# A vision layer's token product in native fp32 throughout, with its 64 tail features once

## What is computed

```
h = einsum('bnd,de->bne', patches(x), W) + b        # 768 -> 192
qkv = h @ w_qkv.T                                   # 192 -> 3 * 768
...
h = _layernorm(h + (scores @ v) @ w_out.T + b_out)
h = _layernorm(h + moe(h))
```

## Time and profile before

| | |
|---|---|
| runs | 155.52 us median (154.16 to 157.65) |
| the profiled execution | 152.08 us, span 150.4 us |
| TensorE busy | 141.0 us, 94% of the span, granted clock 0.995 |
| VectorE, ScalarE, GpSimd busy | 106.0, 95.2, 87.0 us |
| DMA | 10.60 MB, mean 71 GB/s |

### The profile page before, as it was taken

How to read it: one execution, slowest core, us unless ns; L and a number is a source line. 1 busy time by engine, 2 the same in 40 slices (tenths; PEclk the granted TensorE clock), 3 DMA queues, 4 the chain that set the end, 5 groups by cost and what they waited for, 6 DMA issues and landing times. The chain is left out here.

```text
span 150.4 us, 3231 instructions
## 1 busy us (share of the span) xinstructions
PE 141.0 (94%) x1155; PEld 127.3 (85%) x1156; DVE 106.0 (70%) x248; ACT 95.2 (63%) x215; POOL 87.0 (58%) x99
## 2 busy tenths in 40 slices
PE   6999899999999899999979999999999999999960
PEld 2779799999966578798858898999999998999950
DVE  0037889269378879999876538779768797678852
ACT  3055989985498896768688988225555545444531
POOL 7701169590448686899997657737625434433602
PEclk9999999999999999999999999999999999999998
DMA  5899999810033000203300000000000000000021
GB/s 139 261 399 255 247 313 248 226 43 0 3 106 107 2 4 10 97 4 105 109 0 0 0 4 2 0 2 4 0 0 0 0 4 0 0 2 4 0 66 52
DMA packets 4511, 10.60 MB, mean 71 GB/s; under 512 B 592, under 2 KB 1424, under 8 KB 4496
## 3 DMA queue, kind: packets, MB, share of 16 engines
q1 hardware_dynamic: 4496, 10.41, 24.2%
HBM read 9.96 MB, written 0.44 MB: 69 GB/s over the span
## 5 line engine op out<-in xcount | busy, mean ns | idle before, releaser
L462 POOL TENSOR_TENSOR reg_r<-reg_p,reg_r 128x324 fp32r<-128x324 f32 (+1 forms) x23 | 19.1, 832 | 20.6 <-ACT reg_r L721 20.6
L382 POOL TENSOR_TENSOR reg_w<-stage,reg_w 128x768 fp32r<-128x768 f32 x12 | 22.5, 1884 | 12.8 <-DVE reg_q L903 4.5
L721 ACT ACTIVATE reg_r<-reg_p 128x324 fp32r<-128x324 f32 (+1 forms) x24 | 10.6, 443 | 23.9 <-DVE reg_p L1076 23.8
L1053 DVE TENSOR_SCALAR reg_q<-ps,bup 128x324 f32<-128x324 f32 (+1 forms) x24 | 12.3, 513 | 5.3 <-PE ps L1290 5.1
L1076 DVE SCALAR_TENSOR_TENSOR reg_p<-reg_q 128x324 f32<-128x324 f32 (+1 forms) x24 | 13.8, 575 | 2.2
L1286 PE MATMUL ps<-reg_r,reg_w 128*128 128x324 f32 (+1 forms) x48 | 14.9, 311 | 0.0
L1289 PE MATMUL ps<-reg_r,reg_w 128*128 128x324 f32 (+1 forms) x48 | 14.2, 296 | 0.0
L1287 PE MATMUL ps<-reg_r,reg_w 128*128 128x324 f32 (+1 forms) x48 | 14.2, 296 | 0.0
L1290 PE MATMUL ps<-reg_r,reg_w 128*128 128x324 f32 (+1 forms) x48 | 14.2, 296 | 0.0
L1288 PE MATMUL ps<-reg_r,reg_w 128*128 128x324 f32 (+1 forms) x48 | 14.2, 295 | 0.0
L528 ACT ACTIVATE reg_w<-stage 128x768 fp32r<-128x768 f32 x13 | 10.9, 841 | 2.5 <-DMA stage<-w_qkv_a 1.1
(11 more groups left out here) (217 smaller groups left out, 452.6 us busy)
## 6 DMA issues: line engine op xcount, KB each, us to landing
reg_x<-xw_in SPq DMA_DIRECT2D x5, 416.0 KB, 6.4
stage<-w_gu_a SPq DMA_DIRECT2D x4, 384.0 KB, 5.6
stage<-w_gu_b SPq DMA_DIRECT2D x8, 192.0 KB, 3.8
stage<-w_qkv_a SPq DMA_DIRECT2D x3, 384.0 KB, 9.1
stage<-w_qkv_b SPq DMA_DIRECT2D x6, 192.0 KB, 9.2
stage<-w_down SPq DMA_DIRECT2D x3, 384.0 KB, 3.2
wout<-w_out SPq DMA_DIRECT2D x1, 576.0 KB, 11.8
reg_x<-xw_in SPq DMA_DIRECT2D x1, 272.0 KB, 2.8
```

Of the source, the lines that this page charges most:

```text
L382: nc.gpsimd.tensor_tensor(dst[:, 1, :], raw, f(dst[:, 0, :]), ALU.subtract).then_inc(s_wlop, 1)
L462: nc.gpsimd.tensor_tensor(acts[:, n % NACT, 1, 0:w], act_f[:, n % 4, 0:w], f(acts[:, n % NACT, 0, 0:w]), ALU.subtract).then_inc(s_alo, 1)
L1053: nc.vector.tensor_scalar(upw[:, n % 4, 0:w], ps[:, e_bank(n) + 1, 0:w], bup1[:, c:c + 1], LIMIT + 1, ALU.add, ALU.min).then_inc(s_u, 1)
```

## The change

- Chunks 3 to 5 are multiplied natively as well; the split copies `xw`, `x_hi` and `x_lo` go, and so do 36 split products.
- The weights hold the 64 tail columns once: a row has `WX` = 192 + 576 = 768 columns. The tail product of the first token half goes to partitions 0 to 63 of bank 6, that of the second half to partitions 64 to 127 of bank 7, as two products of 64 columns each for every chunk.
- Since each tail half now stands on one half of the partitions only, it is moved when it is evacuated. ScalarE writes the first half's hi in place, the second half's hi in place (partitions 64 to 127, as input of the low part) and once more to partitions 0 to 63; VectorE writes both low parts to partitions 64 to 127, one after the other.
- `hT[:, 0]` is evacuated in two halves: tokens 0 to 287 by ScalarE, 288 to 575 by VectorE, with a semaphore of its own (`s_hthid`). `first_units` goes through token half 0 first and waits for the second half's semaphore before half 1.
- `hb`'s tail has 64 partitions and two instructions; `project`'s second transpose has 64 columns and 64 rows.
- SP issues `small` behind piece 0.

```diff
-XW = T + 2 * 128
+XW = T + D
-WX = 2 * 128
+WX = D
...
-            sp.dma_start(sm[:, :], small).then_inc(s_small, 16)
             for k in range(len(pieces)):
...
+                if k == 0:
+                    sp.dma_start(sm[:, :], small).then_inc(s_small, 16)
...
-            for t in range(2):
-                act.wait_ge(s_tok, t + 1)
-                nc.scalar.activation(two(hT[:, t]), halves(4 + 2 * t), ACT.Identity,
-                                     bias=sm[:, C_TOKB + t:C_TOKB + t + 1]).then_inc(s_hthi, 1)
+            def tail_bias(dst, a, bias):
+
+                r = slice(64 * a, 64 * a + 64)
+                return nc.scalar.activation(dst, ps[r, 6 + a, 0:TH], ACT.Identity, bias=bias[r])
+
+            tail_b = sm[:, C_TOKB + 1:C_TOKB + 2]
+            act.wait_ge(s_tok, 1)
+            nc.scalar.activation(hT[:, 0, 0:TH], ps[:, 4, 0:TH], ACT.Identity, bias=sm[:, C_TOKB:C_TOKB + 1])\
+                .then_inc(s_hthi, 1)
+            act.wait_ge(s_tok, 2)
+            tail_bias(hT[0:64, 1, 0:TH], 0, tail_b).then_inc(s_hthi, 1)
+            tail_bias(hT[64:128, 1, TH:T], 1, tail_b).then_inc(s_hthi, 1)
+            tail_bias(hT[0:64, 1, TH:T], 1, tail_b).then_inc(s_hthi, 1)
...
+            act.wait_ge(s_htlo, 1)
+            act.wait_ge(s_smprep, 3)
+            nc.scalar.activation(two(hb[:, 0]), halves(4), ACT.Identity, bias=tbo[:, 0:1]).then_inc(s_hb, 1)
+            act.wait_ge(s_htlo, 3)
+            tail_bias(hb[0:64, 1, 0:TH], 0, tbo[:, 1:2])
+            tail_bias(hb[0:64, 1, TH:T], 1, tbo[:, 1:2]).then_inc(s_hb, 1)
...
+            dve.wait_ge(s_tok, 1)
+            nc.vector.tensor_scalar(hT[:, 0, TH:T], ps[:, 5, 0:TH], sm[:, C_TOKB:C_TOKB + 1], None, ALU.add)\
+                .then_inc(s_hthid, 1)
+            dve.wait_ge(s_hthid, 1)
             dve.wait_ge(s_hthi, 1)
...
-            dve.wait_ge(s_hthi, 2)
-            nc.vector.scalar_tensor_tensor(out=two(hT[up, 1]), in0=ps[up, 6:8, 0:TH],
-                                           scalar=sm[up, C_TOKB + 1:C_TOKB + 2], in1=two(f(hT[up, 1])),
-                                           op0=ALU.add, op1=ALU.subtract).then_inc(s_htlo, 1)
+            for a in range(2):
+                r = slice(64 * a, 64 * a + 64)
+                cols = slice(TH * a, TH * a + TH)
+                dve.wait_ge(s_hthi, 2 + 2 * a)
+                nc.vector.scalar_tensor_tensor(out=hT[up, 1, cols], in0=ps[r, 6 + a, 0:TH],
+                                               scalar=sm[r, C_TOKB + 1:C_TOKB + 2], in1=f(hT[r, 1, cols]),
+                                               op0=ALU.add, op1=ALU.subtract).then_inc(s_htlo, 1)
...
+                for a in range(2):
+                    last = mm(ps[64 * a:64 * a + 64, 6 + a, 0:TH], xs[:, c, DA:D],
+                              xs[:, c, WX + TH * a:WX + TH * a + TH], start=(c == 0), stop=end)
...
-                for t in range(2):
-                    mm(ps[0:n, L_BANK, DA * t:DA * t + DA], hb[:, t, tok], ident[:, :], start=(t == 0), stop=False,
-                       is_transpose=True, skip_group_check=True)
+                mm(ps[0:n, L_BANK, 0:DA], hb[:, 0, tok], ident[:, :], start=True, stop=False, is_transpose=True,
+                   skip_group_check=True)
+                mm(ps[0:n, L_BANK, DA:D], hb[0:64, 1, tok], ident[0:64, 0:64], start=False, stop=False,
+                   is_transpose=True, skip_group_check=True)
```

More of the change, by code:

```diff
@@ L528, in w_hi @@
                 nc.scalar.activation(dst, raw, ACT.Copy).then_inc(s_whi, 1)
-            for c in range(NAT, NC):
-                x_hi(c)
             w_hi(0)
@@ L840, in _ @@
             nc.vector.memset(small_eps[:, :], NORM_EPS)
-            for c in range(NAT, NC):
-                x_lo(c)
             w_lo(0)
@@ L1256, in _ @@
             keep_warm(6)
-            for c in range(NAT):
+            for c in range(NC):
                 pe.wait_ge(s_x[c], 16)
+                end = c == NC - 1
                 for a in range(2):
@@ L1261, in _ @@
                         pe.wait_ge(s_xb, 16)
-                    for t in range(2):
-                        mm(ps[:, 4 + 2 * t + a, 0:TH], xs[:, c, 128 * t:128 * t + 128],
-                           xs[:, c, WX + TH * a:WX + TH * a + TH], start=(c == 0), stop=False)
-            for c in range(NAT, NC):
-                hi, lo = xw[:, c, 0], xw[:, c, 1]
-                pe.wait_ge(s_xhi, c - NAT + 1)
-                for t in range(2):
-                    for a in range(2):
-                        mm(ps[:, 4 + 2 * t + a, 0:TH], hi[:, 128 * t:128 * t + 128],
-                           hi[:, WX + TH * a:WX + TH * a + TH], start=False, stop=False)
-                pe.wait_ge(s_xlo, c - NAT + 1)
-                for t in range(2):
-                    for wx, px in ((hi, lo), (lo, hi)):
-                        for a in range(2):
-                            last = mm(ps[:, 4 + 2 * t + a, 0:TH], wx[:, 128 * t:128 * t + 128],
-                                      px[:, WX + TH * a:WX + TH * a + TH], start=False,
-                                      stop=(c == NC - 1 and wx is lo))
-                    if c == NC - 1:
-                        last.then_inc(s_tok, 1)
+                    last = mm(ps[:, 4 + a, 0:TH], xs[:, c, 0:DA], xs[:, c, WX + TH * a:WX + TH * a + TH],
+                              start=(c == 0), stop=end)
+                if end:
+                    last.then_inc(s_tok, 1)
+                for a in range(2):
+                    last = mm(ps[64 * a:64 * a + 64, 6 + a, 0:TH], xs[:, c, DA:D],
+                              xs[:, c, WX + TH * a:WX + TH * a + TH], start=(c == 0), stop=end)
+                if end:
+                    last.then_inc(s_tok, 1)
             def wide(bank, w_a, w_b, x, o, n):
@@ L1296, in step @@
                 def step(w, x, start=False):
-                    for m in range(2):
-                        for a in range(2):
+                    for a in range(2):
+                        if start and a == 1:
+                            pe.wait_ge(s_hthid, 1)
+                        for m in range(2):
                             mm(ps[:, slot["qk", m] + a, 0:TH], w[:, 128 * m:128 * m + 128],
@@ L1309, in first_units @@
                 pe.wait_ge(s_w1lo, 1)
-                pe.wait_ge(s_htlo, 2)
+                pe.wait_ge(s_htlo, 3)
                 for m in range(2):
@@ L1715 @@
     w_tok = arr(L0_tok_W).reshape(NC, 128, D)
-    xw = np.concatenate([w_tok, w_tok[:, :, DA:], xT], axis=2)
+    xw = np.concatenate([w_tok, xT], axis=2)
     wqkvT = arr(L0_attn_w_qkv).T.reshape(D, 3, PD).transpose(1, 0, 2)
```

24 lines of the change are left out of this document (4 added, 20 removed).

## The result

| | before | after |
|---|---|---|
| runs (21 of each), median | 154.33 us | 153.71 us |
| ratio of the compared runs | 1 | 1.0058, 95% interval 1.0031 to 1.0085 |
| profiled execution, span | 152.08, 150.4 us | 154.31, 152.6 us |
| TensorE busy | 141.0 us | 142.2 us |
| DMA | 10.60 MB | 10.41 MB |

The changed kernel is 0.9 us slower (0.5 to 1.3 us). The medians stand the other way round because in some executions, more of them of the kernel before, the granted clock is at half for 6.8 us near 80 us, which costs some 3 us; the ratio leaves those out.

The account below looks back on a forecast made before the run. TensorE was taken as the bound (94% of the span), so only an earlier dense stretch counts: 0.6 us from the DMA less 0.15 for an added instruction gives 0.45, from 155.52 to 155.1 us, range 153.0 to 157.2.

Parts of the forecast that it names:

- Rival D: Projection: the five transposes pay the change of array mode, 1.6 us at most, about +0.5 net, 156.0 us; chance 0.08.
- Part 4: Projection: five second hb transposes shrink to 64 columns, 0.03 us each; mode changes taken as costing 0.
- The upper bound of 1.6: Projection: most that five short transposes could cost, up to 2 x 0.16 us each, if 64 rows change the array's mode.
- my own 0.16 for a change: Token products: 0.16 us assumed for each change between whole and divided array.
- Part 3: hT evacuations behind piece 1: one more instruction on the path costs 0.15 us, leaving tail-weight products 0.45 us earlier.
- the overlap of 0.1: VectorE's two hT tail parts, 0.449 us each, were to overlap by 0.1 us as neighbours do now.
- Part 1: Start DMAs: 197 KB less x and small moved behind piece 0; piece 1 lands 0.6 us earlier, 14.6 instead of 15.2.
- Part 2: Token products: 1.78 us a chunk with mode changes, TensorE ready at 14.6, tails at 15.25, off the path.
- Rival B: Token products: pairs do not overlap, 2.26 us a chunk, tail-weight products 1.8 us late, 157.3 us; chance 0.08.
- the margin of 0.3 us: Token stage: TensorE ready at 14.6, ScalarE on piece 1 until 14.92, so TensorE off the path by 0.3 us.
- the cheap case: Token products without cost for mode changes: 1.46 us a chunk, full products end at 13.0, TensorE off the path by 1.8.

Follow-up runs that it names:

- the three with the new order: Changed kernel, full projection transposes, hT ahead of weight-piece splits, late tail products grouped: first 1.0014; mended (table load, one evacuation, DMA order) 0.9964; two waits less 0.9969.
- the first new order: Changed kernel with full transposes, hT ahead of piece 0's split on ScalarE and VectorE, tail products of chunks 2 to 5 together at the end: ratio 1.0014.

## Why the prediction was wrong

The forecast was 0.45 us less, measured is 0.9 us more. Rival D is what happened in the main; I had given it 0.08 and too small a size (0.5).

- **Part 4, the projection, is the step that failed.** I took 0, since L1598 showed that a stationary of 64 columns between full products costs nothing. That row is right (the steps before and behind it are those of its neighbours, 0.15 us at 324 columns and 0.11 to 0.12 at 252), but it has 128 rows and 64 columns; the new transpose has 64 rows, and I let the one stand for the other. It costs three steps of about 0.1 at each projection. In the attention these are three times 0.26, of which 0.26 is regained in the wait behind the first projection and 0.26 in that before the first gate_up product; in the dense stretch 0.29 and 0.24, with no cover, where I had written that it costs nothing. Together 0.8 us, in the trace of after as in that of the edit alone. The upper bound of 1.6 was sound, and my own 0.16 for a change, twice each, was near the truth. Added alone it is 1.0053; taken back it is 1.001, whose interval decides nothing by itself, but the steps in its traces are those of before. The Trainium skill, TensorEngine Tiling (Array Packing), Tiling Modes, says that changing the mode drains the engine. The short transposes and the pairs of the token stage agree with that; L1598, which has a shape of its own between full products and loses nothing, does not. Which shapes count as a change stays open.
- **Part 3, the evacuations, was mis-sized:** +0.50 and not +0.15, from 2.90 to 3.40 between piece 1 and the tail products. Up to VectorE's low part of the whole features the steps held: 1.34 us behind piece 1 (15.53 to 16.87) where I had 1.30 and before shows 1.08. The term that failed is the two tail parts, 1.06 us and not 0.80: each takes 0.51 to 0.52 and not the 0.449 of L1061, an instruction of another kind (its output is f32), and the overlap of 0.1 that I took off is not there where a wait stands between the two. The last 0.09 is in small parts.
- **Part 1, the DMA, was right in the mean and small beside its scatter.** (A chunk's row has `XW` = 192 + 576 = 768 columns after the change; `WX`, the weights alone, is 192.) Piece 1 starts at 15.20, 14.99, 16.47, 16.21 and 15.54 in the five executions with before's rows (mean 15.7), at 14.93, 15.53, 15.65, 14.19 and 14.03 in the five with the narrow rows and after's order of transfers (mean 14.9). That is 0.8 between samples that each spread over 1.5; the direct measure gives 0.4 to 0.5.
- **Part 2, the token products, was right.** The pairs run together (0.71 us for four records, 0.64 from their first to the next line), from chunk to chunk it is 1.80 (9.87, 11.67, 13.47), predicted 1.78, and the tails are done at 15.35 (15.25). Rival B is out. That the tails end within 0.1 of the forecast is in part luck: I had carried the slow first chunk over from one trace, and how long it takes differs by 1 us between executions. So the margin of 0.3 us was not one: where piece 1 came at 14.19 and 14.03, ScalarE waited 1.09 and 0.69 us for these products, and part of the DMA's gain is cut off. (In the cheap case the margin is 14.92 less 13.0, 1.9 and not 1.8; nothing hangs on it.)

The front together: the tail products start at 18.10, 17.94, 19.37 and 19.12 with the old front (mean 18.6; the one with the tail in two is left out), at 18.32, 18.93, 19.05 and 18.03 with the new one (mean 18.6; the one with one evacuation is left out). The scores of the attention come at 42.9 in the mean of either four. As far as so few executions tell, the front gains nothing and loses nothing; 0.8 us at the projections is then nearly the whole of the 0.9 that was measured, and the 0.2 in the last part of the kernel, which both traces of after show, stands within the interval too. The 0.8, the 0.35 of part 3 and this 0.2 add up to the 1.35 between forecast and measurement, more evenly than the scatter of the front allows one to claim. In the two executions at the top the front differs by 0.84: 0.50 behind piece 1, and 0.33 in its landing, which I count as scatter. How much of the DMA's gain is cut off on the average stays open.

## What to carry to other kernels

A product that uses half of the array's rows or columns is not to be priced by its work, and not by a row of a similar shape either. Here one with 128 rows and 64 columns between full ones cost nothing, pairs of such cost 0.34 us a visit, and one with 64 rows 0.29; so find a row with the same rows, columns and neighbours, or measure one. In a stretch where the engine has no idle time such a change counts in full. When a transfer gates a start, measure how far its landing, and what stands ready just behind it, scatter between executions before forecasting a gain of that size, since the second cuts the gain off. When work is moved off a busy engine, the chain that ends last is to be followed through each single instruction with its own partitions and columns.

## What the runs showed of the hardware

- **Changes of the array's division.** From four full records to a pair of half width and back cost 0.34 us in a chunk: 1.80 us less six steps of 0.243. In a row without changes the sixteen records of four chunks' tails take 2.09 us from the first to the next line, 0.13 a record. A transpose with 64 rows between full products costs 0.26 to 0.29 us; L1598, 128 rows and 64 columns without a partner, costs nothing.
- **VectorE waits for GpSimd to end, and so the phase decides.** From the last gate_up product to the start of the last product it is 4.32 or 4.33 us in eight traces, those of before and of the full transposes among them, and 4.53 to 4.55 in six: both of after, the three with the new order, and the kernel before with its tail in two. VectorE's L1076 on 252 columns takes 0.42 us alone, 0.63 in the trace of before, where it starts 0.38 us behind GpSimd's L462, and 0.91 in after, where it starts 0.09 behind it:

```profile
142.72 0.91 DVE L1076 SCALAR_TENSOR_TENSOR reg_p<-reg_q 128x252 f32<-128x252 f32 x1
```
```profile
142.63 0.73 POOL L461 TENSOR_TENSOR reg_r<-reg_p,reg_r 128x252 fp32r<-128x252 f32 x1
```

In all 48 places of the 14 traces where this instruction starts well inside GpSimd's, it ends 0.27 to 0.28 us behind the end of GpSimd's, whether it started 0.09 or 0.55 us into it. A shift of a few tenths of a microsecond of the whole program decides how much is lost. The last part does not go with either kernel: both traces of after have the long one, but so has the kernel before with its tail in two, and after with the full transposes does not. I did not try to steer it.
- **ScalarE's table load** (1.28 us) stands directly in front of the first ACTIVATE. It did not wait for the one semaphore that this ACTIVATE waits for: in before it runs at 0.80 us and the ACTIVATE at 9.09, in after at 0.80 and 12.51. With two waits in front (the first new order) the second is an instruction of its own, at 12.38, and the load came behind it at 12.43, on the path.
- **TensorE's first products.** In all 14 traces they run at half their later pace at first (steps of 0.48 us instead of 0.243), until some time between 4.1 and 7.3 us. With that the token stage ends up to 1 us earlier or later.
- **The clock behind an idle stretch.** TensorE idle for 1.80 us, and the granted clock at half from 1.5 us behind the restart on, for 3.4 us. In the kernel before with the short transpose TensorE idled 1.68 us at the same place and the clock stayed at 1.00. That is one trace each; that the idle time is the cause is not shown.
